# An adaLN attention and routed feed-forward block: the feed-forward matmuls on f32 operands instead of split f16 ones

## The reference

```
h = layernorm(x) * (1 + ca) + sa
x = x + ga * attention(h)            # 16 heads over channels, softmax over 1024
h = layernorm(x) * (1 + cb) + sb
scores = h @ w_router                # one score a token
top_idx = top_k(scores, 512)         # half of each batch's tokens
sel = h[top_idx]                     # 512 x 512
f = gelu(sel @ W1 + b1)              # W1 is 512 x 2048
p = f @ W2 + b2                      # W2 is 2048 x 512
h[top_idx] += sigmoid(top_scores) * p
x = x + gb * h
```

## Time and profile before

| | us |
|---|---|
| median of 3 runs | 2440.17 |
| lowest, highest | 2437.55, 2441.03 |
| the profiled execution, in all | 2431.43 |
| its span in the profile | 2429.7 |
| PE busy | 2272.0 (94%) |
| DVE busy | 1903.2 (78%) |
| ACT busy | 1477.5 (61%) |
| POOL busy | 1367.7 (56%) |
| first feed-forward matmul starts | 1691.53 |

### The profile page before, as it was taken

The page is one execution under the profiler, slowest core; times in us unless marked ns, Lnnn a source line. Parts: engine busy times, 40 slices in busy tenths (PEclk is TensorE's granted clock), DMA queues, the critical chain, the costliest instruction groups (busy, mean ns, idle before and its releaser), DMA issues.

```text
span 2429.7 us, 41301 instructions
## 1 busy us (share of the span) xinstructions
PE 2272.0 (94%) x12772; PEld 886.5 (36%) x12772; DVE 1903.2 (78%) x2806; ACT 1477.5 (61%) x2616; POOL 1367.7 (56%) x1205
## 2 busy tenths in 40 slices
PE   7999999999999999999999999877689999999996
PEld 2333333333333333333333333222244444444443
DVE  5899999999999999999999999988444543553432
ACT  1788888888888888878888888767211111111110
POOL 4566676667666666667666675553344452443531
PEclk9999999999999999999999999999899999999998
DMA  6233333232333334233333334223312012011100
GB/s 212 69 91 78 78 87 85 68 96 67 81 95 75 74 77 101 68 79 83 79 81 90 77 71 101 64 60 110 108 44 66 22 48 62 28 61 44 54 25 18
DMA packets 123771, 180.83 MB, mean 74 GB/s; under 512 B 44112, under 2 KB 44112, under 8 KB 123480
## 3 DMA queue, kind: packets, MB, share of 16 engines
q1 hardware_dynamic: 113760, 152.30, 25.0%
q0 software_dynamic: 9728, 25.23, 3.4%
HBM read 67.17 MB, written 43.16 MB: 45 GB/s over the span
## 4 chain that ended last, share of the span: by engine, by line
PE 65%; DVE 16%; issue 9%; POOL 4%; ACT 3%; DMA 1%; SPq 1%; DVEq 0%; POOLq 0%; ACTq 0%
PE sc L552 13%; PE sc L741 13%; PE acc L599 13%; PE sc L728 12%; DVE nmax L976 9%; PE pj L562 8%; PE pj L574 5%; POOL x L1314 3%; DVE qn L1037 2%; ACT probs L804 2%; DVE stats L1019 1%; PE sc L585 1%; PE sc L614 1%; DVE rinv L1032 0%; DMA room<-in_L_ffn_W 0%
## 5 line engine op out<-in xcount | busy, mean ns | idle before, releaser
L804 ACT ACTIVATE probs<-sc,nmax 128x1024 f32<-128x1024 f32 x1024 | 1136.7, 1115 | 272.5 <-DVE nmax L976 254.8
L976 DVE TENSOR_REDUCE nmax<-sc 128x1 f32<-128x1024 f32 x1024 | 1212.1, 1215 | 57.0 <-PE sc L552 51.4
L599 PE MATMUL acc<-probs,qn 128*32 128x512 f32 x4136 | 554.6, 609 | 3.3 <-DVE qn L1037 2.3
L878 ACT ACTIVATE probs<-sc,b_col 128x512 f32<-128x512 f32 x128 | 87.8, 687 | 552.2 <-PE sc L728 552.1
L562 PE MATMUL pj<-room 128*128 128x512 f16 x1536 | 395.3, 381 | 0.4 <-ACT qT L794 0.4
L741 PE MATMUL sc<-room,probs 128*128 128x512 f16 x1536 | 354.7, 381 | 26.8 <-DVE probs L1165 26.8
L552 PE MATMUL sc<-room 128*128 128x512 f16 x1024 | 309.4, 384 | 40.7 <-ACT probs L804 24.1
L552 PE MATMUL sc<-stacks 128*128 128x512 f16 x1024 | 309.6, 384 | 38.3 <-ACT probs L804 37.7
L1163 DVE CAST probs<-probs 128x512 f16<-128x512 f32 x128 | 62.5, 489 | 356.3 <-ACT probs L878 356.1
L741 PEld LDWEIGHTS sc<-room,probs 128*128 128x128 f16 x1536 | 150.3, 98 | 209.8 <-DVE probs L1165 27.6
L562 PEld LDWEIGHTS pj<-room 128*128 128x128 f16 x1536 | 150.1, 98 | 188.4 <-issue 8.9
(11 more groups left out here) (147 smaller groups left out, 2361.1 us busy)
## 6 DMA issues: line engine op xcount, KB each, us to landing
room<-room SPq DMA_DIRECT2D x512, 64.0 KB, 2.0
stacks<-room SPq DMA_DIRECT2D x512, 64.0 KB, 2.0
h_rows<-hbuf SPq DMA_DIRECT2D x132, 128.0 KB, 2.4
out<-base SPq DMA_DIRECT2D x132, 128.0 KB, 2.6
room<-in_L_attn_x SPq DMA_DIRECT2D x96, 128.0 KB, 2.5
rows<-mod_rows SPq DMA_DIRECT2D x32, 256.0 KB, 4.0
room<-in_L_ffn_W SPq DMA_DIRECT2D x8, 1024.0 KB, 6.1
probs<-in_L_wmod SPq DMA_DIRECT2D x4, 1024.0 KB, 7.8
```

What stands on the lines that cost most here:

```text
L599: mm = nc.tensor.matmul(acc[at:at + DH, :], qn[:, (p // 2) % 2, p % 2, h2, :], probs[:, (2 * p + h2) % PROBS, half * D:(half + 1) * D], st ...
L804: nc.scalar.activation(probs[:, u % PROBS, :], slot(g, ring_at(p, h2)), ACT.Exp, bias=nmax[:, u % PROBS:u % PROBS + 1], accum_out=rsum[:, ...
L878: nc.scalar.activation(g32[:, f % 2, :], ff[f % 2], ACT.Gelu_apprx_tanh, bias=b1_col[:, f:f + 1], scale=1.0 / WS).then_inc(gelu_done, 1)
L976: nc.vector.tensor_reduce(nmax[:, u % PROBS:u % PROBS + 1], slot(g, ring_at(p, h2)), AX.X, ALU.max, negate=True).then_inc(max_done, 1)
```

## The change

The feed-forward takes its operands in f32 as they are. The eight pieces of W1 and W2 are loaded straight to their place, in the same bytes that the high and low parts had (`w1_32`, `w2_32`), and stage, `high_part` and `low_part` go. ff1 and ff2 have one f32 matmul where three f16 ones were, so four a part instead of twelve. The gelu's output is used directly. ACT copies a transposed chunk of the kept rows in one go (`kept_out`), and the low parts (`kept_low`) go. The pieces of weights are all loaded in the last attention group, ahead of the last stores of rows. The transposes of batch 0's kept rows move from pairs 8, 10, 12, 14 to 6, 9, 12, 14 of that group. The ranking of batch 0 is cut into smaller parts, put at more pairs, and ends four pairs earlier; half of its stores are issued earlier.

```diff
-                if j >= 2:
-                    sp.wait_ge(w_lo, j - 1)
-                sp.dma_start(stage[:, j % 2], src).then_inc(s_stage[j], 16)
+                sp.dma_start(dst, src).then_inc(s_stage[j], 16)
...
                     if last and g == GB - 1:
                         load_kept(0, 0)
-                        sp.wait_ge(t_pe, NG)
+                        sp.wait_ge(q_evac, 2 * NG)
                         load_weights(0)
+                        for k in range(2):
+                            for s in range(SUBS):
+                                sp.wait_ge(s_stk[k][1][s], stk_count(LAST, GB - 1))
+                        load_weights(1)
                     sp.wait_ge(x2_done, b * GB + g + 1)
...
-                        load_weights(1)
-                        load_weights(2)
+                        for j in range(2, 8):
+                            load_weights(j)
...
                 if f % 4 == 0:
-                    pe.wait_ge(w_lo, 2 * (f // 4) + 1)
-                terms = [(cc, a, z) for cc in range(CC) for z, a in ((0, 0), (0, 1), (1, 0))]
-                for t, (cc, a, z) in enumerate(terms):
-                    mm = nc.tensor.matmul(ff[f % 2], w1_16[:, z, cc, f * P:(f + 1) * P], fT16[par][a][:, cc, :],
-                                          start=(t == 0), stop=(t == len(terms) - 1))
+                    pe.wait_ge(s_stage[2 * (f // 4)], 16)
+                for cc in range(CC):
+                    mm = nc.tensor.matmul(ff[f % 2], w1_32[:, cc, f * P:(f + 1) * P], fT[par][cc],
+                                          start=(cc == 0), stop=(cc == CC - 1))
...
-                pe.wait_ge(g_split, n_of(bb, par, FC, f + 3))
+                pe.wait_ge(gelu_done, n_of(bb, par, FC, f + 3))
                 for kt in range(KT):
-                    for t, (a, z) in enumerate(((0, 0), (0, 1), (1, 0))):
-                        mm = nc.tensor.matmul(ff2[kt], g16[:, f % 2, a, kt * P:(kt + 1) * P], w2_16[:, z, f, :],
-                                              start=(f == 0 and t == 0), stop=(f == FC - 1 and t == 2))
+                    mm = nc.tensor.matmul(ff2[kt], g32[:, f % 2, kt * P:(kt + 1) * P], w2_32[:, f, :],
+                                          start=(f == 0), stop=(f == FC - 1))
...
-                        if end and p == 3:
...
-                            high_part(0)
-                        if end and p == 8:
-                            high_part(1)
-                        if end and p == 12:
-                            high_part(2)
-                        if end and p > NQ and p % 2 == 1:
-                            kept_high(0, 0, (p - NQ) // 2, aux[0])
+                        if end and p - 1 in KEPT_AT:
+                            kept_out(0, 0, KEPT_AT.index(p - 1), aux[0])
...
-                    dve.wait_ge(gelu_done, n_of(bb, par, FC, f + 3))
-                    nc.vector.tensor_copy(g16[:, f % 2, 0, :], g32[:, f % 2, :]).then_inc(g_hi, 1)
-                    dve.wait_ge(g_hi, n_of(bb, par, FC, f + 1))
-                    nc.vector.tensor_tensor(g16[:, f % 2, 1, :], g32[:, f % 2, :], g16[:, f % 2, 0, :], ALU.subtract).then_inc(g_split, 1)
...
+                    if last and g == GB - 2:
+                        wait_alone(r.s_slot, 1)
+                        store_kept(nc, r, sel_rows, range(0, TB // 4))
```

More of the change, by code:

```diff
@@ L86, in count_above @@
                                 accum_out=r.before[:, t:t + 1]).then_inc(r.s_cmp, 1)
+def count_above(nc, dve, r, t, count):
+    own = t * P
     nc.vector.tensor_scalar(r.cmp_out[:, own:T], r.srow[:, own:T], r.s8[:, t:t + 1], 0.0, ALU.is_gt, ALU.add,
@@ L205, in block_phases @@
         pj = pb("pj", [P, D])
[L207 to L209 removed]
+        w1_32 = room1[:].bitcast(F32).rearrange("p (c n) -> p c n", c=CC)
+        w2_32 = room2[:].bitcast(F32).rearrange("p (f n) -> p f n", f=FC)
         b1_col = sb("b1_col", [P, FC], F32)
@@ L213, in block_phases @@
         kept_i = sb("kept_i", [P, 2, KT], I32)
[L214 to L219, removed]
+        f_b0 = sb("f_b0", [P, 2, KEEP], F32)
+        f_a0 = qT[0][:].rearrange("p (a c) n -> p a (c n)", a=2)
+        late = stacks[1][:].rearrange("p k h n -> p (k h n)").bitcast(F32).rearrange("p (k n) -> p k n", n=KEEP)
+        fT = [[f_a0[:, 0], f_a0[:, 1], f_b0[:, 0], f_b0[:, 1]], [late[:, cc] for cc in range(CC)]]
+        hs = [k_bias[:], late[:, CC:2 * CC]]
         spare = probs[:].rearrange("p u (i n) -> p (u i) n", n=D)
@@ L679, in body @@
                         if end:
-                            if p >= NQ and p % 2 == 0:
-                                cc = (p - NQ) // 2
+                            if p in KEPT_AT:
+                                cc = KEPT_AT.index(p)
                                 if cc == 0:
@@ L817, in _, with kept_out @@
             evac_q(0, 1, 2)
[L818 to L827, removed]
+            def kept_out(bb, par, cc, src):
                 act.wait_ge(ft_pe, n_of(bb, par, CC, cc + 1))
-                nc.scalar.activation(fT16[par][0][:, cc, :], src, ACT.Identity).then_inc(ft_hi, 1)
+                nc.scalar.activation(fT[par][cc], src, ACT.Identity).then_inc(ft_done, 1)
             def body(b, last):
@@ L842, in body @@
                             evac_q((g + 1) % 2, (p - 13) // 2, n2 + (p - 13) // 2 + 1)
[L843 removed]
+                        if last and g == 1 and p == 0:
                             act.wait_ge(s_dot, 2 * (NG - 3))
                             nc.scalar.activation(r.e_neg[:, 0:LAST * TB], scores[:, 2:2 + LAST * TB], ACT.Exp, scale=-1.0).then_inc(s_exps, 1)
[L846 to L856 removed]
+                        if end and p - 1 in KEPT_AT:
+                            kept_out(0, 0, KEPT_AT.index(p - 1), aux[0])
                         no_entry = last and g >= GB - 2
@@ L1054, in weights @@
                 nc.vector.reciprocal(r.tokens[:, part, 1], r.e_neg[:, part]).then_inc(s_tok, 1)
-            def low_part(j):
-                k = j // 2
-                dve.wait_ge(w_hi, j + 1)
-                if j % 2 == 0:
-                    hi, lo = (w1_16[:, z, :, k * D:(k + 1) * D] for z in range(2))
-                else:
-                    hi, lo = (w2_16[:, z, 4 * k:4 * (k + 1), :] for z in range(2))
-                nc.vector.scalar_tensor_tensor(out=lo, in0=stage[:, j % 2], scalar=WS, in1=hi, op0=ALU.mult,
-                                               op1=ALU.subtract).then_inc(w_lo, 1)
             def numbers(bb, par):
@@ L1108, in body @@
                         row_max(b, g, p, 0)
+                        if end and p == 2:
+                            numbers(0, 0)
                         if p == 3:
@@ L1130, in body @@
                             rank_first(g, p)
-                        if end and p == 1:
-                            numbers(0, 0)
-                        if end and p == 7:
-                            low_part(0)
-                        if end and p > NQ and p % 2 == 1:
-                            kept_low(0, 0, (p - NQ) // 2, aux[0])
             with dve.Fori(0, B - 1) as b:
@@ L1221, in ffn @@
                 for kt in range(KT):
-                    nc.vector.scalar_tensor_tensor(out=y[par][:, kt, :], in0=ff2[kt], scalar=1.0 / WS, in1=b2_row,
-                                                   op0=ALU.mult, op1=ALU.add).then_inc(acc_out, 1)
+                    nc.vector.tensor_tensor(y[par][:, kt, :], ff2[kt], b2_row, ALU.add).then_inc(acc_out, 1)
                 if not last:
@@ L1403, in body @@
                     if last and g == GB - 2:
-                        wait_alone(r.s_slot, 1)
-                        store_kept(nc, r, sel_rows, range(0, TB // 2))
+                        store_kept(nc, r, sel_rows, range(TB // 4, TB // 2))
                     behind_qn(b, g, 7)
```

133 lines of the change are left out of this document (35 added, 98 removed).

## The result

The kernel after took 2600.7 us (median of 4 runs, 2599.19 to 2602.89), the kernel before beside it 2438.86 us (4 runs, 2436.71 to 2441.03). The ratio is 1.066, 95% interval 1.065 to 1.068: slower by 162 us, where 162.5 were forecast. The profiled execution was 2599.56 us with a span of 2597.8.

What follows compares the result with a forecast made beforehand. PE's own work was taken to bound the feed-forward: +213.5 for f32 matmuls, -24.9, -10.8 and -4.3 for waits, -11 for the last attention group, +162.5 on 2440.17, so 2603 us; stated range 2580 to 2645.

Steps and rivals of the forecast that it cites:

- The main term: Feed-forward matmuls: four f32 ones take 3.42 us a part against 2.59 for twelve f16, 256 parts, 213.5 us more.
- Weight loads at nothing: Feed-forward: 2048 full-width f32 weight loads overlap with neighbouring work and cost nothing; upper bound 307 us.
- Three waits, 40.0 us: PE's feed-forward waits go: third ff2 24.9 us, gather at step 12 10.8, low part at batch borders 4.3.
- 9 us of cover: Step 12 of the feed-forward: gathered rows ready at 76.2 us, first transposes wanting them after 85.6 us.
- The last attention group, 11 us: The last attention group, 61.0 us long, gets 11 us shorter as DVE and ACT lose work; bounds 4.5 and 12.5.
- The ranking spread, 0 with 3 us either way: Batch 0's ranking is spread over more pairs but not less work: 0, with 3 us either way.
- the carried difference: Timed runs' median lay 8.7 us above the profiled execution before; this was added to the forecast for the kernel after.
- A: Rival: f32 weight loads in the feed-forward are not hidden, 225 us more, 2828 us (2910 at whole duration); chance 0.09.
- B: Rival: full-width f32 feed-forward matmuls stream like the transposes, 0.44 us each, 1.76 us a part, 2209 us; chance 0.04.
- C: Rival: eight weight loads in one go delay the pair 6 gather and SP's later stores, 12 us, 2615 us; chance 0.05.

Runs made afterwards that it cites:

- e_thin_w: The kernel after with weights of 32 columns instead of 128 in all 1024 feed-forward matmuls; 2609.15 us (one run).
- e_short_move: The kernel after with 128 moving columns instead of 512 in all 1024 feed-forward matmuls, weights of full width; 2152.93 us (one run).
- b_loads: The kernel before with the loads of weight pieces 4 and 5 put ahead of SP's wait for the last stores; 2420.72 us, ratio 0.992 to the kernel before.
- late loads: The kernel after with weight pieces 3 to 7 loaded where the kernel before has them; 2603.86 us, then 2602.5 beside 2601.34 for the kernel after.
- e_old_rank: The kernel after with batch 0's ranking, its stores and its exponential at the kernel before's pairs; 2600.28 us, ratio 1.066 to the kernel before.

## Why the prediction was right

- **The main term.** Forecast 3.42 us a part, +213.5 us; measured 3.43 us. The reading of one group in the setup as two records of two passes carried over to full-width weights. The estimate from the four passes of the Trainium skill ("FP8 and Floating Point Precision", TensorE Precision Notes), 3.45 us a part, agrees with the trace's 3.43.
- **Weight loads at nothing.** Right: e_thin_w shows no change of a part by width, e_short_move hides a load even in 111 ns. The load lasts 190 ns, not the 150 taken from the transposes, which made no difference. The Trainium skill's sentence that loads overlap only where the row group differs ("TensorE: Matmul & The Clock Gate", Part 3, The mechanism) doesn't hold here: all loads of the phase are of the full array and none is exposed. The same section also lets loads into a background weight buffer run ahead; no run here shows which way these loads take.
- **Three waits, 40.0 us.** All gone; the phase was forecast at 892 us and took 892.0. For the longest, b_loads shows the cause by removing it without touching the arithmetic. One link of the forecast's chain was wrong there, though its gain was right: it had the load wait for a free stage, while the stage was free 24 us before the load went out and SP's wait for the last stores held it. It was also the fourth ff2 that waited (1734.94 us, behind those at 1696.72, 1701.90 and 1707.08), not the third. The gain came all the same, since in the kernel after no gelu stands behind a piece of weights; the late loads, with SP's old order, show no wait either. That the gather at step 12 is in time was forecast with 9 us of cover. It had more: the stores of numbers began at 1715.35 us, 29.6 us after the phase began, against the 51.3 assumed, as DVE's counts no longer stand behind splits.
- **The last attention group, 11 us.** Mis-sized in this pair of profiles: the last group alone lost 8.5 us (61.0 to 52.5), the last batch's attention 7.7. The step that failed is that the wait for the kept tokens' numbers goes since the stores begin earlier: the eighth store, which the load waits for, still follows on base_plus at the end of group 2 (1634.29 us), and 3.8 of the 4.5 us remained. Against the slower attention of b_loads the gain is 9.8 us and more, so how far 11 was off stays open.
- **The whole, 2603 against 2600.7.** Partly luck. Between the two profiled executions the difference is 168.1 us, 5.6 more than forecast (3.3 in the last batch's attention, 1.8 ahead of it, 0.2 in the phase, 0.3 left over). Between the medians it is 2600.7 - 2438.86 = 161.8. The forecast carried over that before's profiled execution lay 8.7 us below its median; after's lay only 1.1 below (2599.56 against 2600.7). So the steps were 5.6 us too low and the carried difference 7.6 us too high.
- **The ranking spread, 0 with 3 us either way.** Right by e_old_rank in the whole (2600.28 against 2600.7 us), though 6 us late in the middle.
- **Rivals.** A fell with e_thin_w. B fell with the result, and e_short_move shows why its reading of the transposes misled. Of C, the eight loads in one go, nothing was seen: PE has no wait for gathered rows in the last group, and late loads gain nothing.

## What to carry to other kernels

Count TensorE's passes before anything else: where PE has no gaps, one f32 matmul (four passes) in place of three f16 ones is a third more time (3.43 against 2.59 us a part), however much splitting it takes off the other engines. If the splits are what hurts, look first for the one transfer that stands behind an unrelated wait in its queue: here moving two loads gave 18 us with the arithmetic untouched. And read a price from rows of the same kind of operation: the transposes gave the right answer for weight loads and half the right one for products.

## What the runs showed of the hardware that was not expected

- Changing between narrow weights (8 or 32 columns) and full-width ones costs 0.10 to 0.14 us each time: 3.53 instead of 3.43 us for four f32 matmuls before transposes, 0.58 instead of 0.44 us for the transposes (e_thin_w). At the change from narrow to wide the first wide load isn't run ahead; between loads of full width it is. Why was not tried.
- A full-width f32 weight load is recorded with 190 ns ahead of products and 141 to 150 ns ahead of transposes, and neither is exposed down to a record every 111 ns. A load of 32 columns still lasts 110 ns (e_thin_w).
- In b_loads PE ran at the lower clock behind a wait of only 2.8 us: granted 0.63 over the next 4.04 us.
